# Attention block on one core: the row maxima's matmuls regrouped, three in a step and a round of four after every fourth

## The chip, the core and the metric

The kernel runs on one core of a Trainium2 chip. A time is the device time of one execution in microseconds. All engines of the core run at once: TensorE (matmuls; "PE" in the profile, its weight loads "PEld"), VectorE (DVE), ScalarE (ACT), GpSimd (POOL) and SyncE (SP, which issues most of the transfers). Each takes its instructions in the order of its program and waits at semaphores for the others.

## The reference

A transformer block with conditioning, two sequences of 2048 rows, width 512, 16 heads of 32:

```python
h = _ln(x) * (1.0 + scale_msa) + shift_msa
q = (h @ Wq + bq).reshape(B, L, H, DH)
k = (h @ Wk + bk).reshape(B, L, H, DH)
v = (h @ Wv + bv).reshape(B, L, H, DH)
scores = jnp.einsum('blhe,bshe->bhls', q, k)
A = jax.nn.softmax(scale * scores, axis=-1)
out = jnp.einsum('bhls,bshd->blhd', A, v)
x = x + gate_msa * (out @ Wo + bo)
h2 = _ln(x) * (1.0 + scale_mlp) + shift_mlp
m = jax.nn.gelu(h2 @ W1 + b1, approximate=False) @ W2 + b2
return x + gate_mlp * m
```

The change touches the scores, the softmax and the product with `v` only.

## The kernel before

Three stages: layer norm and the projections to q, k, v (to about 370 us), attention over 32 heads (16 of each sequence; to about 1975 us), then the output projection and the MLP. The projections and k and q are kept as a high and a low half, so that a product has three or more matmuls.

**A head of attention.** `G` is 32 heads, `NT` 16 steps. A step `t` takes 128 keys (on the partitions) against all 2048 queries (four quarters of 512, `r` = 0 to 3). For every quarter there is one score tile, S0 to S3, 128 x 512 in one bank of PSUM. It is the sum of four matmuls, its parts p0 to p3: high by high (line 1373), low by high (1375), high by low (1377), and minus the maximum of each query (1382). Each uses 32 rows of TensorE's array, quarter `r` the row group `r`, so that up to four of different quarters run together. ScalarE then takes the exponential of S0 to S3 (line 888), four a step. TensorE multiplies the probabilities of the step before by `v` ("values", line 1397) into bank 7.

**Max tiles.** The maximum of a query must be known before its exponentials. So in each step the kernel also computes score tiles of the next head the other way round (queries on the partitions, high halves only): the max tiles M0 to M3 (`max_tile`, line 1361), one matmul each, again in row group `r`. VectorE reduces each to one column of `part_max` (`quad`, line 1096); after the last of a head it reduces these columns to the row maxima and transposes them (lines 1043, 1049), and SyncE puts them in place for the next head.

**Sums.** The softmax's denominators are column sums of the probabilities. GpSimd adds up eleven of the sixteen tiles (`pool_tiles`: 0, 1, 3, 4, 6, 7, 9, 10, 12, 13, 14), twenty additions a head (line 737). TensorE sums the other five (2, 5, 8, 11, 15) and GpSimd's total, with four matmuls against ones each (line 1386): six groups a head, after the values, in steps 3, 6, 9, 12, in step 0 of the next head, and in step 4. ScalarE copies each out (line 866) and stores it. In step 0 it first copies the output of the head before (line 854), which waits for the same sums group. In step 8 VectorE makes the reciprocals of the denominators of the head before (lines 1106, 1108), after the step's reductions.

**Order in a step (TensorE).** Five slots of four matmuls of different row groups:
slot 0: p0 of S0 and S1, M2, M3; slot 1: p1 of S0 and S1, p0 of S2 and S3; slot 2: p2, and p1; slot 3: p3, and p2; slot 4: M0, M1, p3 of S2 and S3. Then values, then a sums group if the step has one. VectorE reduces in the order M2, M3, M0, M1.

**Banks.** Scores, max tiles and sums share seven banks of PSUM. `bank_table` (lines 87 to 131) walks the program in TensorE's order with estimated times of release (`until`, in units of its own) and gives each tile the bank that comes free first. It is a table made ahead; at run time the first matmul into a bank waits for what read it last (`bank_free`): `exp_ok` (ScalarE's exponential), `a_max` (VectorE's reduction) or `sums_ok` (ScalarE's copy). In the table of the head I looked at (head 10), M1 always gets the bank of M2 of the same step.

```python
elif kind == "M":
    pe.wait_ge(a_max, n)
```

Of the kernel before, what the change touches and what calls it, by code (L numbers as in the profile page):

```python
# [21 lines left out]
ALU = mybir.AluOpType  # L22
ACT = mybir.ActivationFunctionType
AX = mybir.AxisListType
# [10 lines left out]
TT = CH // P  # L35
CPB = L // CH
NCHUNK = B * CPB
G = B * H
NT = L // P
NQ = L // CH  # L40
# [7 lines left out]
FILLS = NQ * NT  # L48
LEAD = 3
FIRST_QUADS = 4  # L50
# [36 lines left out]
def bank_table():  # L87

    step, group = 11.7, 3.7
    until = {"S": (8, 10, 12, 14), "M": (11, 13, 6, 8), "D": 16}
    free = [0] * BANKS
    last = [None] * BANKS
    count = {"S": 0, "M": FIRST_FILLS, "D": 0}
    last[BANKS - 1] = ("M", FIRST_FILLS - 1)

    def use(kind, at, banks):
        bank = min(banks, key=lambda b: free[b])  # L100
        free[bank] = at
        before = last[bank]
        count[kind] += 1
        last[bank] = (kind, count[kind])
        return bank, before, count[kind]

    now = 0
    heads = []
    for g in range(G):
        steps = []  # L110
        for t in range(NT):
            tail = g == G - 1
            banks = range(BANKS)
            uses = {"max": [None] * NQ, "scores": [None] * NQ, "sums": []}
            for pair, others in ((0, 1), (2, 3)), ((2, 3), (0, 1)):
                for r in pair:
                    uses["scores"][r] = use("S", now + until["S"][r], range(3 + r, 4 + r) if tail else banks)
                if (g or t) and g < G - 2 or g == G - 2 and t < NT - LEAD:
                    for r in others:
                        uses["max"][r] = use("M", now + until["M"][r], banks)  # L120
            owner = g if t else g - 1
            groups = [(owner, pe_tiles(owner).index((t - 1) % NT))] if owner >= 0 and (t - 1) % NT in pe_tiles(owner) else []
            if g and t == ACC_STEP:
                groups.append((g - 1, ND - 1))
            for n, (o, d) in enumerate(groups):
                uses["sums"].append((o, d, *use("D", now + until["D"] + 2 * n, range(2, 3) if tail else banks)))
            now += step + group * len(groups)
            steps.append(uses)
        heads.append(steps)
    end = [(G - 1, d, *use("D", now, range(2, 3))) for d in (ND_MOST - 2, ND_MOST - 1)]  # L130
    return heads, end
# [8 lines left out]
def block_kernel(nc, x, cT, wq, wk, wv, wo, w1, w2, wada, bqT, bkT, b1T, badaT, bada, bv, bo, b2, out):  # L140
# [8 lines left out]
    with ExitStack() as ctx:  # L149
# [11 lines left out]
        ps = ctx.enter_context(nc.psum_tensor("ps", [P, 8, 512], F32))  # L161
# [39 lines left out]
        sums = [view(work, at, CH) for at in (3072, 1024)]  # L201
# [93 lines left out]
        a_mm = sem("a_mm")  # L295
# [651 lines left out]
        def _(dve):  # L947
# [89 lines left out]
            def row_maxima(g):  # L1037
                dve.wait_ge(a_max, (g + 1) * FILLS)
                if not isinstance(g, int) or g:
                    dve.wait_ge(maxT_ok, g)  # L1040
                else:
                    dve.wait_ge(zero_ok, 1)
                nc.vector.tensor_reduce(row_max[:, 0:NT], part_max[:], AX.X, ALU.max).then_inc(max_ok, 1)

            def transpose_max(g):
                dve.wait_ge(max_ok, g + 1)
                if not isinstance(g, int) or g:
                    dve.wait_ge(maxT_in, g * (16 * MAX_PIECES))
                nc.vector.transpose(max_T[:], row_max[:]).then_inc(maxT_ok, 1)
# [39 lines left out]
            chunk(NCHUNK - 1, 1, CPB - 1, nxt=False, nxt2=False, max_after=FIRST_MAX[NCHUNK - 1], max_at=MAX_AT_7)  # L1089
            assert next(fills, None) is None  # L1090

            def quad(uses, g, q):

                for r, (bank, _, n) in zip((2, 3, 0, 1), uses):
                    dve.wait_ge(a_mm, n)
                    nc.vector.tensor_reduce(part_max[:, r * TT + q // NQ, q % NQ:q % NQ + 1], ps[:, bank, :], AX.X, ALU.max).then_inc(a_max, 1)  # L1096
                if q == FILLS // NQ - 1:
                    row_maxima(g)
                    transpose_max(g)

            def denominators(g):

# [6 lines left out]

            def head(g, between={}):  # L1110

                q = g * (FILLS // NQ) + (LEAD if g else FIRST_QUADS)
                for t, uses in enumerate(USES[g]):
                    if uses["max"][0]:
                        quad([uses["max"][r] for r in (2, 3, 0, 1)], 1 + q // (FILLS // NQ), q % (FILLS // NQ))
                        q += 1
                    if t == STEP_RECIP and g:
                        denominators(g - 1)
                    if t in between:
                        between[t]()  # L1120
# [107 lines left out]
        def _(pe):  # L1228
# [126 lines left out]
            def max_tile(g, q, r, use):  # L1355


                bank_free(use)
                u = g % HI_BUF
                at = slice(r * DH, (r + 1) * DH)  # L1360
                nc.tensor.matmul(ps[:, use[0], :], q_hi[u][at, q // NQ * P:(q // NQ + 1) * P],  # L1361
                                 k_hi[u][at, q % NQ * CH:(q % NQ + 1) * CH], start=True, stop=True).then_inc(a_mm, 1)
# [48 lines left out]

            def head(g, between={}):

                per_head = FILLS // NQ
                q = g * per_head + (LEAD if g else FIRST_QUADS)
                pe.wait_ge(lo_in[g % TWO], (g // TWO + 1) * (16 * LOADS_LO))
                for t, uses in enumerate(USES[g]):
                    scores, tops = uses["scores"], uses["max"]
                    if tops[0] and q % per_head == 0:
                        ahead = 1 + q // per_head  # L1420
                        pe.wait_ge(hi_in[ahead % HI_BUF], (ahead // HI_BUF + 1) * (16 * LOADS_HI))
                    for part in range(5):
                        if part < 4:
                            score_part(g, t, 0, part)
                            score_part(g, t, 1, part)
                        if part:
                            if part == 4 and tops[0]:
                                for r in (0, 1):
                                    max_tile(1 + q // per_head, q % per_head, r, tops[r])
                            score_part(g, t, 2, part - 1)  # L1430
                            score_part(g, t, 3, part - 1)
                        elif tops[0]:
                            for r in (2, 3):
                                max_tile(1 + q // per_head, q % per_head, r, tops[r])
                    if tops[0]:
                        q += 1
                    if t:
                        values(g, t - 1)
                    elif g:
                        values(g - 1, NT - 1)  # L1440
                    take_sums(uses["sums"])
                    if t in between:
                        between[t]()
# [114 lines left out]
```

## Time and profile before

| | |
|---|---|
| median of 3 runs | 2422.54 us (2421.5 to 2427.32) |
| profiled execution: time | 2425.6 us |
| its span | 2423.8 us |
| mean granted TensorE clock | 0.989 |
| busy TensorE / VectorE / ScalarE / GpSimd | 2362.5 / 1743.6 / 1403.8 / 1656.4 us |
| attention, 700 to 1680 us (980 us): the same four | 978.5 / 809.4 / 744.4 / 943.6 us |

The busy time of TensorE counts matmuls that run together and their modelled ends, so it does not show how tightly its queue is filled; for that one reads when each instruction starts. Idle time is shown as [idle, what ended it]. The attention stage repeats the same pattern head for head, so a few steps stand for all.

### The profile page before, as it was taken

To read this page: it belongs to the slowest core of one execution; us is meant where nothing else is said; L and a number is where in the kernel's file an instruction comes from. 1 tells how busy PE (TensorE), PEld (TensorE's weight loads), DVE (VectorE), ACT (ScalarE), POOL (GpSimd) and SP (SyncE) were. 2 spreads that over 40 slices of the span, in tenths; PEclk is the share of its full clock that TensorE was granted. 3 is DMA by queue.
4 is the path that set the end of the run, shared out by engine and by line. 5 is a ranking of instruction groups with operands and counts; after the bars stand their busy time and mean duration, and the time that the engine had idled before them with its cause. 6 is when DMAs were issued, how large, how long until landed. Compare 5 with 4: busy or idle time off the path is not lost.

```text
span 2423.8 us, 48535 instructions
## 1 busy us (share of the span) xinstructions
PE 2362.5 (97%) x19312; PEld 1341.3 (55%) x19312; DVE 1743.6 (72%) x2866; ACT 1403.8 (58%) x2591; POOL 1656.4 (68%) x776
## 2 busy tenths in 40 slices
PE   6999989999999999999999999999999889999998
PEld 4787764444444444444444444444444458888887
DVE  5445747888888888888888888888888656655653
ACT  3232216777777777777777777777777642222221
POOL 0000017999999999999999999999999842233320
PEclk9999999999999999999999999999999989999999
DMA  8666463332333323232323223322323223222200
GB/s 282 192 195 185 133 165 76 69 82 65 70 80 72 75 64 82 57 82 56 80 57 82 56 67 70 75 63 60 77 59 75 68 70 94 70 70 70 70 35 35
DMA packets 208845, 211.14 MB, mean 87 GB/s; under 512 B 116253, under 2 KB 149021, under 8 KB 199081
## 3 DMA queue, kind: packets, MB, share of 16 engines
q1 hardware_dynamic: 206338, 206.41, 32.8%
q8 instruction: 152, 2.49, 0.4%
q10 hardware_dynamic: 2280, 1.63, 0.3%
q14 instruction: 75, 0.61, 0.1%
HBM read 147.11 MB, written 60.59 MB: 86 GB/s over the span
## 4 chain that ended last, share of the span: by engine, by line
PE 91%; ACT 2%; DMA 2%; DVE 2%; issue 2%; SPq 1%; POOL 0%; ACTq 0%; POOLq 0%; DVEq 0%
PE ps L1397 21%; PE ps L1258 19%; PE ps L1373 11%; PE ps L1361 11%; PE ps L1501 7%; PE ps L1386 7%; PE ps L1375 6%; PE ps L1377 5%; PE ps L1382 3%; DMA q_lo<-work 1%; PE ps L1267 1%; ACT work L866 1%; PE ps L1299 1%; DVE acts_r L1136 0%; ACT work L802 0%
## 5 line engine op out<-in xcount | busy, mean ns | idle before, releaser
L1096 DVE TENSOR_REDUCE part_max<-ps 128x1 f32<-128x512 f32 x1968 | 1221.5, 682 | 265.2 <-PE ps L1361 265.2
L888 ACT ACTIVATE work<-ps 128x512 f32<-128x512 f32 x2048 | 1057.8, 603 | 324.1 <-PE ps L1382 281.9
L737 POOL TENSOR_TENSOR work<-work 128x1024 f32<-128x1024 f32 x314 | 739.8, 2412 | 37.8 <-ACT work L888 37.3
L737 POOL TENSOR_TENSOR gate<-gate,work 128x1024 f32<-128x1024 f32 x288 | 675.1, 2404 | 14.4 <-ACT work L888 14.4
L1397 PE MATMUL ps<-work 128*32 128x512 f32 x4096 | 546.4, 605 | 0.1
L1361 PE MATMUL ps<-acts_r 32*128 32x512 f32 x1328 | 412.6, 471 | 3.3 <-ACT work L888 1.8
L1258 PE MATMUL ps<-acts_r,weights_r 128*128 128x512 f32 x1536 | 382.7, 399 | 4.6 <-DVE acts_r L1013 3.9
L1258 PEld LDWEIGHTS ps<-acts_r,weights_r 128*128 128x128 f32 x1536 | 291.1, 192 | 70.8 <-issue 6.4
L1373 PEld LDWEIGHTS ps<-acts_r 32*128 32x128 f32 x1408 | 141.2, 182 | 305.1 <-DVE part_max L1096 175.2
L1373 PE MATMUL ps<-acts_r 32*128 32x512 f32 x1408 | 291.4, 466 | 1.4 <-issue 0.8
L1375 PE MATMUL ps<-acts_r 32*128 32x512 f32 x1408 | 252.7, 394 | 0.0
L1361 PEld LDWEIGHTS ps<-acts_r 32*128 32x128 f32 x1328 | 179.8, 182 | 109.9 <-DVE part_max L1096 89.1
L941 ACT ACTIVATE work<-ps,b_sb 128x512 f32<-128x512 f32 x64 | 44.2, 690 | 333.0 <-PE ps L1258 333.0
L709 POOL TENSOR_TENSOR var_eps<-var_eps,mv 128x4 f32<-128x4 f32 x16 | 3.2, 202 | 338.5 <-DVE mv L991 338.5
L1382 PE MATMUL ps<-acts_r,minus_r 1*128 1x512 f32 x1024 | 228.8, 441 | 0.0
L1382 PE MATMUL ps<-m_odd,minus_r 1*128 1x512 f32 x1024 | 225.6, 438 | 0.0
L761 POOL TENSOR_TENSOR work<-work,gate_b 128x512 f32<-128x512 f32 x60 | 86.4, 1470 | 169.8 <-DMA work<-in_x 149.4
L1258 PE MATMUL ps<-weights_r,acts_r 128*128 128x512 f32 x768 | 191.6, 401 | 8.9 <-DVE acts_r L1136 8.9
L1361 PE MATMUL ps<-acts_r,w_r 32*128 32x512 f32 x640 | 198.6, 470 | 0.8
L1386 PE MATMUL ps<-work,ones 128*32 128x512 f32 x1432 | 187.3, 595 | 0.0
L1377 PE MATMUL ps<-w_r,acts_r 32*128 32x512 f32 x1024 | 184.6, 394 | 0.0
L1501 PE MATMUL ps<-w_r,acts_r 128*128 128x512 f32 x768 | 184.4, 391 | 0.0
(95 smaller groups left out, 2808.1 us busy)
## 6 DMA issues: line engine op xcount, KB each, us to landing
acts_r<-k_hi SPq DMA_DIRECT2D x130, 256.0 KB, 4.7
acts_r<-k_lo SPq DMA_DIRECT2D x129, 256.0 KB, 4.7
work<-in_x SPq DMA_DIRECT2D x16, 1024.0 KB, 6.1
q_hi<-work SPq DMA_DIRECT2D x32, 256.0 KB, 3.1
q_lo<-work SPq DMA_DIRECT2D x32, 256.0 KB, 3.5
k_hi<-work SPq DMA_DIRECT2D x32, 256.0 KB, 2.6
k_lo<-work SPq DMA_DIRECT2D x32, 256.0 KB, 3.2
v_rows<-work SPq DMA_DIRECT2D x32, 256.0 KB, 2.0
```

What stands on the lines that cost most here:

```text
L737: nc.gpsimd.tensor_tensor(acc[:, at], first, prob[:, t % RING, at], ALU.add).then_inc(add_ok, 1)
L888: nc.scalar.activation(prob[:, t % RING, j * CH:(j + 1) * CH], ps[:, bank, :], ACT.Exp, scale=SCALE).then_inc(exp_ok, 1)
L1096: nc.vector.tensor_reduce(part_max[:, r * TT + q // NQ, q % NQ:q % NQ + 1], ps[:, bank, :], AX.X, ALU.max).then_inc(a_max, 1)
L1258: mm = nc.tensor.matmul(o, lhs(s, kk), rhs(r, kk), start=(kk == 0 and s == r), stop=(kk == KC - 1 and s == 1))
L1361: nc.tensor.matmul(ps[:, use[0], :], q_hi[u][at, q // NQ * P:(q // NQ + 1) * P], k_hi[u][at, q % NQ * CH:(q % NQ + 1) * CH], start=True, s ...
L1373: nc.tensor.matmul(o, k_hi[u][at, keys], q_hi[u][at, :], start=True, stop=False)
L1375: nc.tensor.matmul(o, k_lo[w][at, keys], q_hi[u][at, :], start=False, stop=False)
L1377: nc.tensor.matmul(o, k_hi[u][at, keys], q_lo[w][at, :], start=False, stop=False)
L1382: nc.tensor.matmul(o, minus_r[row, :], m_row[w][row, :], start=False, stop=True).then_inc(b_mm, 1)
L1386: mm = nc.tensor.matmul(ps[j * DH:(j + 1) * DH, bank, :], ones[:, 0:DH], src(j), start=True, stop=True)
L1397: mm = nc.tensor.matmul(ps[j * DH:(j + 1) * DH, O_BANK, :], v_sb[g % TWO][:, t, :], prob[:, t % RING, j * CH:(j + 1) * CH], start=(t == 0) ...
L1501: mm = nc.tensor.matmul(ps[:, 4 + t, :], g_r[:, f % 4, s, t * P:(t + 1) * P], w2_r[:, r, f, :], start=(f == 0 and s == r), stop=(f == FB - ...
```

## The change

The four max tiles of a step (a "round" in the code; rounds are numbered through all heads, `FIRST_QUADS` of them made ahead) become three: tile `r` equal to the round's number modulo 4 is left out. In a step of a head after the first the round's number modulo 4 is (t + 3) modulo 4: steps 1, 5, 9, 13 leave out M0, steps 2, 6, 10, 14 M1, steps 3, 7, 11, 15 M2, steps 0, 4, 8, 12 M3. In the latter the four tiles left out in the last four steps follow after the values and ahead of a sums group, as four matmuls together, here called L0 to L3. VectorE takes them after the step's three; row maxima and, in step 8, denominators follow them. The number of max tiles is the same. The bank table is made anew by the same rule, with estimates for L0 to L3. The short description of the change also speaks of TensorE summing tile 7 in place of 8; the code leaves `pool_tiles` as it was.

```diff
@@ bank_table
-            uses = {"max": [None] * NQ, "scores": [None] * NQ, "sums": []}
+            uses = {"round": None, "max": [None] * NQ, "late": [], "scores": [None] * NQ, "sums": []}
+            if (g or t) and g < G - 2 or g == G - 2 and t < NT - LEAD:
+                uses["round"] = next(rounds)
...
-                if (g or t) and g < G - 2 or g == G - 2 and t < NT - LEAD:
+                if uses["round"] is not None:
                     for r in others:
-                        uses["max"][r] = use("M", now + until["M"][r], banks)
+                        if r != uses["round"] % NQ:
+                            uses["max"][r] = use("M", now + until["M"][r], banks)
+            if uses["round"] is not None and uses["round"] % NQ == NQ - 1:
+                uses["late"] = [use("M", now + 15 + 2.8 * r, banks) for r in range(NQ)]
+                now += 2.6
...
@@ VectorE, head
-                    if uses["max"][0]:
-                        quad([uses["max"][r] for r in (2, 3, 0, 1)], 1 + q // (FILLS // NQ), q % (FILLS // NQ))
-                        q += 1
+                    if uses["round"] is not None:
+                        q = uses["round"] % NT
+                        for r in (2, 3, 0, 1):
+                            if uses["max"][r]:
+                                tile_max(q, r, uses["max"][r])
+                        for r, use in enumerate(uses["late"]):
+                            tile_max(q - (NQ - 1) + r, r, use)
+                        if q == NT - 1:
+                            row_maxima(1 + uses["round"] // NT)
+                            transpose_max(1 + uses["round"] // NT)
...
@@ TensorE, head
                     if t:
                         values(g, t - 1)
                     elif g:
                         values(g - 1, NT - 1)
+
+                    for r, use in enumerate(uses["late"]):
+                        max_tile(ahead, q - (NQ - 1) + r, r, use)
                     take_sums(uses["sums"])
```

What stands in TensorE's queue at two places of head 10. A row is line, operation, tile written and read, and in brackets the semaphore that it waits for; L1373 is the first part of a score, L1361 a max tile, L1397 the values, L1386 a sums group (after: L1383, L1371, L1407, L1396). First, the end of step 8 and the begin of step 9, before:

```order
L1397 MATMUL ps<-work 32x512 [waits exp_ok]
L1397 MATMUL ps<-work 32x512 x3
L1373 MATMUL ps<-acts_r 128x512 [waits exp_ok]
L1373 MATMUL ps<-acts_r 128x512 [waits a_max]
L1361 MATMUL ps<-acts_r,w2_r 128x512 [waits exp_ok]
L1361 MATMUL ps<-acts_r,w2_r 128x512 [waits a_max]
L1375 MATMUL ps<-acts_r 128x512 x2
L1373 MATMUL ps<-acts_r 128x512 [waits exp_ok]
L1373 MATMUL ps<-acts_r 128x512 [waits a_max]
```

And after:

```order
L1407 MATMUL ps<-work 32x512 [waits exp_ok]
L1407 MATMUL ps<-work 32x512 x3
L1371 MATMUL ps<-acts_r,w2_r 128x512 [waits a_max]
L1371 MATMUL ps<-acts_r,w2_r 128x512 [waits exp_ok] x2
L1371 MATMUL ps<-acts_r,w2_r 128x512 [waits a_max]
L1383 MATMUL ps<-acts_r 128x512 [waits exp_ok]
L1383 MATMUL ps<-acts_r 128x512 [waits a_max]
L1371 MATMUL ps<-acts_r,w2_r 128x512 [waits exp_ok]
L1371 MATMUL ps<-acts_r,w2_r 128x512 [waits a_max]
L1385 MATMUL ps<-acts_r 128x512 x2
L1383 MATMUL ps<-acts_r 128x512 [waits a_max] x2
L1387 MATMUL ps<-w2_r,acts_r 128x512 x2
```

The round L0 to L3 stands between the values and step 9, and both first parts of S2 and S3 (the last but one row) now wait for reductions: by the table S2 for that of L1, S3 for that of M2 of step 9 itself. Before, S3 waited for M0 of step 8.

Second, the begin of step 1, behind the sums group of step 0, before:

```order
L1386 MATMUL ps<-work,ones 32x512 x3
L1373 MATMUL ps<-acts_r 128x512 [waits a_max]
L1373 MATMUL ps<-acts_r 128x512 [waits exp_ok]
L1361 MATMUL ps<-acts_r,w2_r 128x512 [waits exp_ok]
L1361 MATMUL ps<-acts_r,w2_r 128x512 [waits a_max]
L1375 MATMUL ps<-acts_r 128x512 x2
L1373 MATMUL ps<-acts_r 128x512 [waits exp_ok]
L1373 MATMUL ps<-acts_r 128x512 [waits a_max]
```

And after:

```order
L1396 MATMUL ps<-work,ones 32x512 x3
L1383 MATMUL ps<-acts_r 128x512 [waits a_max]
L1383 MATMUL ps<-acts_r 128x512 [waits exp_ok]
L1371 MATMUL ps<-acts_r,w2_r 128x512 [waits a_max] x2
L1385 MATMUL ps<-acts_r 128x512 x2
L1383 MATMUL ps<-acts_r 128x512 [waits sums_ok]
L1383 MATMUL ps<-acts_r 128x512 [waits a_max]
```

M2 and M3 wait for reductions (L0 and L1), S2 in slot 1 for the copy of the sums group of step 0, S3 for L2. Before, the wait for that copy stood at M0, in slot 4.

## Rows read from the trace of the kernel before

**Rows 1.** Waits, 700 to 1700 us: engine, line, releaser: us, times, longest.

```profile
PEld ps L1361 <- DVE part_max L1096: 88.4, 283, 0.5
```

**Rows 2.** One step in order of time: start, us, engine, line, operation, tiles, count, [idle].

```profile
1004.20 0.50 PE L1373 MATMUL ps<-acts_r 32*128 32x512 f32 x2
...
1004.54 0.40 PE L1375 MATMUL ps<-acts_r 32*128 32x512 f32 x2
...
1004.75 2.48 DVE L1096 TENSOR_REDUCE part_max<-ps 128x1 f32<-128x512 f32 x4 [0.24 <-PE ps L1361]
...
1005.00 0.40 PE L1382 MATMUL ps<-acts_r,minus_r 1*128 1x512 f32 x2
...
1005.24 0.75 PE L1361 MATMUL ps<-acts_r,w_r 32*128 32x512 f32 x2
1005.49 0.18 PEld L1361 LDWEIGHTS ps<-acts_r,w_r 32*128 32x128 f32 x1 [0.30 <-DVE part_max L1096]
...
1005.50 0.49 PE L1382 MATMUL ps<-acts_r,minus_r 1*128 1x512 f32 x2
1005.92 1.06 PE L1397 MATMUL ps<-work 128*32 128x512 f32 x8
...
1006.92 0.49 PE L1373 MATMUL ps<-acts_r 32*128 32x512 f32 x2
```

**Rows 3.** VectorE: the cost of one reduction; denominators in step 8; row maxima.

```profile
L1096 DVE TENSOR_REDUCE part_max<-ps 128x1 f32<-128x512 f32 x1968 | 1221.5, 682 | 265.2 <-PE ps L1361 265.2
...
1038.12 0.31 DVE L1106 TENSOR_REDUCE den_c<-sums_c 128x16 f32<-128x96 f32 x1
...
1038.64 2.41 DVE L1096 TENSOR_REDUCE part_max<-ps 128x1 f32<-128x512 f32 x4
...
1050.11 0.22 DVE L1043 TENSOR_REDUCE row_max<-part_max 128x16 f32<-128x64 f32 x1
1050.37 0.21 DVE L1049 STREAM_TRANSPOSE max_T<-row_max 128x32 f32<-128x32 f32 x1
```

**Rows 4.** GpSimd's additions in a row; copies of three heads' outputs, first and last start.

```profile
1031.25 32.77 POOL L737 TENSOR_TENSOR work<-work 128x1024 f32<-128x1024 f32 x14 [0.46 <-ACT work L888]
...
L854 ACT ACTIVATE work<-ps x3: 598/600/600, 1013.4 to 1111.6; 128x512 f32<-128x512 f32 x3
```

**Rows 5.** Sums groups and ScalarE's copies, step 0 to 1 and step 3.

```profile
1012.24 1.04 PE L1386 MATMUL ps<-work,ones 128*32 128x512 f32 x8
1013.22 0.50 PE L1373 MATMUL ps<-acts_r 32*128 32x512 f32 x2
...
1013.35 0.60 ACT L854 ACTIVATE work<-ps 128x512 f32<-128x512 f32 x1 [0.30 <-PE ps L1386]
1013.85 0.59 ACT L866 ACTIVATE work<-ps 128x512 f32<-128x512 f32 x1
...
1020.65 1.06 PE L1397 MATMUL ps<-work 128*32 128x512 f32 x8
1021.53 1.04 PE L1386 MATMUL ps<-work,ones 128*32 128x512 f32 x8
...
1022.64 0.60 ACT L866 ACTIVATE work<-ps 128x512 f32<-128x512 f32 x1 [0.36 <-PE ps L1386]
```

**Rows 6.** Step 8: S2's first part after a hold, and its second.

```profile
1035.68 0.50 PE L1373 MATMUL ps<-acts_r 32*128 32x512 f32 x2
...
1035.78 0.19 PEld L1375 LDWEIGHTS ps<-acts_r 32*128 32x128 f32 x2
...
1036.01 0.39 PE L1375 MATMUL ps<-acts_r 32*128 32x512 f32 x2
```

**Rows 7.** The start of attention: a long hold; windows (last: PEclk, DMA share, GB/s).

```profile
370.11 0.51 PE L1373 MATMUL ps<-acts_r 32*128 32x512 f32 x4 [0.83 <-issue]
...
373.31 0.79 PE L1361 MATMUL ps<-acts_r 32*128 32x512 f32 x1 [1.75 <-ACT work L888]
...
372.00:379.00 7.00, 5.69 (x33) 2.70 (x37) 2.27 (x4) 4.78 (x9) 2.19 (x1) 0.54 0.77 173
```

More of the change, by code:

```diff
@@ L107, in bank_table @@
     now = 0
+    rounds = iter(range(FIRST_QUADS, G * NT))
     heads = []
@@ L1090, in _, with tile_max @@
             assert next(fills, None) is None
[L1092 to L1099, printed above, removed]
+            def tile_max(q, r, use):
+                bank, _, n = use
+                dve.wait_ge(a_mm, n)
+                nc.vector.tensor_reduce(part_max[:, r * TT + q // NQ, q % NQ:q % NQ + 1], ps[:, bank, :], AX.X, ALU.max).then_inc(a_max, 1)
             def denominators(g):
@@ L1110, in head @@
             def head(g, between={}):
-                q = g * (FILLS // NQ) + (LEAD if g else FIRST_QUADS)
                 for t, uses in enumerate(USES[g]):
-                    if uses["max"][0]:
-                        quad([uses["max"][r] for r in (2, 3, 0, 1)], 1 + q // (FILLS // NQ), q % (FILLS // NQ))
-                        q += 1
+                    if uses["round"] is not None:
[8 more added lines that the diff above has]
+                            transpose_max(1 + uses["round"] // NT)
                     if t == STEP_RECIP and g:
@@ L1412, in head @@
             def head(g, between={}):
-                per_head = FILLS // NQ
-                q = g * per_head + (LEAD if g else FIRST_QUADS)
                 pe.wait_ge(lo_in[g % TWO], (g // TWO + 1) * (16 * LOADS_LO))
@@ L1418, in head @@
                     scores, tops = uses["scores"], uses["max"]
-                    if tops[0] and q % per_head == 0:
-                        ahead = 1 + q // per_head
+                    ahead, q = (1 + uses["round"] // NT, uses["round"] % NT) if uses["round"] is not None else (0, 0)
+                    if ahead and q == 0:
                         pe.wait_ge(hi_in[ahead % HI_BUF], (ahead // HI_BUF + 1) * (16 * LOADS_HI))
@@ L1426, in head @@
                         if part:
-                            if part == 4 and tops[0]:
+                            if part == 4:
                                 for r in (0, 1):
-                                    max_tile(1 + q // per_head, q % per_head, r, tops[r])
+                                    if tops[r]:
+                                        max_tile(ahead, q, r, tops[r])
                             score_part(g, t, 2, part - 1)
                             score_part(g, t, 3, part - 1)
-                        elif tops[0]:
+                        else:
                             for r in (2, 3):
-                                max_tile(1 + q // per_head, q % per_head, r, tops[r])
-                    if tops[0]:
-                        q += 1
+                                if tops[r]:
+                                    max_tile(ahead, q, r, tops[r])
                     if t:
```

## The prediction

> **What bounds the kernel now.** I read the waits first, then one step on all engines in order of time, then the length of a head. In the waits of the middle stretch [rows 1] TensorE's weight loads for max tiles (line 1361) are held 283 times by VectorE, 88.4 us in all, 0.3 us each. One step [rows 2] shows which: S0 of the step starts at 1004.20; the p1 slot follows 0.34 later, p3 of S0 at 1005.00 (0.80), M0 at 1005.24 (1.04). M1 should go with M0, but sits in the bank of M2 of the same step, whose reduction began at 1004.75 and needs 0.68 [rows 3]; M1 goes at 1005.49, and since TensorE issues in order p3 of S2 and S3 goes at 1005.50. Values follow 0.42 later (1005.92), the next step 1.00 after that: 2.72 us. Without the hold it is 1.04 + 0.42 + 0.99 = 2.45. So TensorE's in-order stream sets the end, lengthened by bank waits. Behind it VectorE is close: four reductions take 2.48 [rows 2], 0.60 apart. GpSimd is closer: 14 additions take 32.77, 2.35 each [rows 4]; a head has 20, 47.1 us of a head of (1111.6 - 1013.4) / 2 = 49.1 [rows 4]. A head cannot get shorter than 47.1.
>
> **What the change removes.** With three max tiles in a step, none sits in the bank of M2 of its own step when M1 comes: I went through the bank table of head 10, and in it M1 never follows M2 of the same step. Sixteen holds of 0.27 go, 4.3 us a head, and with them 0.4 of scattered waits in the head before (49.1 less 16 steps of 2.72 and six sums groups of 0.86). The 0.86: values to sums is 0.88, sums to the next S0 0.98 [rows 5], together 1.86 in place of 0.99. A head without any bank wait would be 16 x 2.45 + 6 x 0.86 = 44.4. A slot with three matmuls in place of four is taken at the same price: the slots are spaced 0.23 to 0.24 by each row group's own next matmul.
>
> **What it adds: the round.** Four matmuls of their own, after values, in steps 0, 4, 8 and 12 of a head (123 rounds in the kernel). TensorE changes from values to 32-row matmuls (0.99), from these to the sums group (0.43, as from slot 4 to values [rows 2]), instead of 0.88 straight: 0.54 more in steps 0, 4 and 12, where a sums group follows. Step 8 has none: 0.34 (the distance of the first two slots [rows 2]). Sum 1.96 a head.
>
> **What it adds: waits behind the round.** VectorE gets seven tiles in a round's step. L0's reduction starts 0.54 after the round (as M2's after S0 [rows 2]), the others 0.60 apart, each ready 0.68 after its start and its bank taken 0.06 later (reduction from 1004.75, M1 at 1005.49). The step that follows wants these banks early, in slots 0 and 1, and TensorE's queue holds all score parts behind. Counted from S0 of the following step:
> Step 5 (after step 4): M3 waits for L1, 0.34; S2 for the sums group's copy, 0.81 (sums matmul to copy 1.11, copy 0.60 [rows 5], S0 0.97 after the sums); S3 for L2, 0.94. Then p1 at 1.27, p2 1.50, p3 1.74 (0.33 after a hold, as from 1035.68 to 1036.01 [rows 6], then 0.23 and 0.24). M1 waits for L3, 1.54, and is hidden. Step 3.16, 0.71 over the clean 2.45.
> Step 13: the round is 0.14 later against S0, S3 at 1.08: 3.30, 0.85 over. VectorE then also does the row maxima (0.22 and 0.21 [rows 3]); its M1 is late enough to hold S3 of step 14 until 0.76: 0.53 over.
> Step 1: ScalarE copies the head's output before the sums (1013.35, then 1013.85 to 1014.44, which is 1.22 after S0 at 1013.22 [rows 5]). Before, M0 in slot 4 wanted this bank (1.04 at the earliest); now S2 in slot 1 does, and goes at 1.30: p3 2.10, step 3.52, 1.07 over.
> The round's own steps want S3's bank from an exponential of the step before (ready 0.52 to 0.57 into the step instead of 0.34): 0.28 to 0.34 in steps 0, 8 and 12, and 0.14 in step 4 where the sums wait for S2's exponential. With small rests 1.1. Together 1.1 + 0.71 + 0.85 + 0.53 + 1.07 = 4.3.
> For the 0.33 after a hold there is another reading. In the row, the load for p1 of S2 starts at 1035.78, 0.10 after its matmul p0, and the matmul comes at 1036.01 [rows 6]. The Trainium skill ("TensorE: Matmul & The Clock Gate", "Step-by-step: what each phase is for") says that weight loads are pulled ahead of matmuls in flight where row groups don't conflict or into a background buffer; by it the queue would restart at 0.23, and eight holds a head would cost 0.8 less, 25 us in all. I stay with the row.
>
> **What it adds: one long wait.** In step 9 the table gives S3 (slot 1) the bank of M2 (slot 0) of the same step, as it gave M1 that bank before; but now the hold comes in slot 1, and M2's reduction stands behind the whole round and the denominators. The round of step 8 goes 2.79 after its S0 and S0 of step 9 at 3.13. Reductions: L0 3.33, L3 5.13, then the denominators in place of 5.73, which cost 0.52 (1038.12 to 1038.64 [rows 3]), M2 at 6.25, done 6.93. S3 goes at 6.99, 3.86 into step 9; until then all that is queued (p2, p3, values, sums) waits. p3 4.66, values 5.09, sums 5.97, step 6.94 instead of 2.45 + 0.86 = 3.31: 3.63 over. The table has this in step 9 of every head from 0 to 30.
>
> **Sum.** 44.4 + 1.96 + 4.3 + 3.63 gives 54.2 a head (with the pieces unrounded) for 49.1: 5.1 more. Steps with max tiles are 492 (1968 reductions by 4), 30.75 heads: 157 us. The profiled execution is 2423.8 of span and 2425.6 in time; 2425.6 + 157 = 2583. The median of the runs is 3 lower.
>
> **The clock.** TensorE idles 1.8 us in each step 9 (S2's first matmul, begun at 1.54 and 0.50 long, to 3.86). After a wait of 1.75 (with another of 0.83 shortly before) the clock fell: 372 to 379 ran at 0.54 [rows 7], and lost 7 x 0.46 = 3.2 us. The holds of 0.3 never lowered it. The new wait is nearest to the 1.75, but without a second one near it, so between 0 and 31 x 3.2 = 99 us; I take a third, 33. That makes 2616 of the profiled, **2613** as a median.
>
> **Rivals.**
> *The intended gain.* If banks were free by the time they are wanted after a round, a head would be 44.4 + 2.0 = 46.4, and GpSimd's 47.1 would decide; some 47.5 with its own waits, 1.6 less x 30.75: 2374. It needs the step 9 hold to be no hold; VectorE's order and the table speak against it. Chance 0.06.
> *Only step 9 counts.* The smaller waits hide beneath one another and the restart costs 0.23: 44.4 + 2 + 3.6 and about 1 is 51, 1.9 more a head, 2480 to 2530. It is slower all the same; it would turn to no change only where the small waits and half of step 9's went. 0.12.
> *The clock falls in every step 9.* 2583 + 99 = 2682, median about 2680; slow matmuls would then show in every head. 0.15.
> *The change as its words say.* Tile 7 is not summed by TensorE: the list of tiles is untouched, the sums group stays in step 9. If it moved to step 8, the table would hand S3 of step 9 the bank of L2, the 3.6 would shrink to about 1.3, and the time to about 2510. The code decides against it, and it has no chance of its own.
> *A second queue.* GpSimd, held back by the long step 9, makes ScalarE wait in steps 10 to 15. In my walk its addition for tile 14 ends 2 us before it is wanted again, so 0.04, above 2700.
>
> **How the numbers follow.** Forecast (step 9 long, small waits as walked, the clock down in some heads) 0.59; the rest as above, and 0.04 for something between gain and no change. Range 2510 to 2690: from the second rival's upper part to the clock's, beyond which lie 0.06 + 0.04 + 0.04 and a few hundredths of the second. A measurement of this kernel tells 0.3% (7 us) from no change: faster 0.08, within 0.04, slower 0.88.
>
> **What would show it.** Heads 54 us long or more by the copies of the output; one step in a head of 7 us, with TensorE's line for S3 held by VectorE near 2.3 us; clean steps of 2.45 (2, 7, 10) with no hold at M1; steps 1, 5, 13 of 3.2 to 3.5; steps 0 and 12 near 4.1; GpSimd's share down from 96% of a head to 87%. VectorE's reductions keep 0.60. Wrong, if step 9 is under 5 us, if the matmuls of a round don't go together, or if clean steps stay at 2.72.

## The result, and the profile after

The changed kernel takes 2603.54 us by the median of five runs, the kernel before 2422.54, also by five: a ratio of 1.0744 with an interval of [1.0721, 1.0767]. It is 181 us slower; 2613 was forecast. One of the five executions, the profiled one, took 3724.65 us at a mean granted clock of 0.555, which was down from some 34 us on, long before the changed part, for a reason that the runs don't show; it stands in no comparison. The profile shown here is of another run of the same kernel (e1_after, 2602.19 us median of 4).

| | before | after (e1_after) |
|---|---|---|
| span of the profiled execution | 2423.8 | 2601.6 |
| mean granted clock | 0.989 | 0.967 |
| a head, by the copies of the output | 49.1 | 54.7 |
| VectorE idle before reductions, all | 265.2 | 419.5 |
| GpSimd idle before additions, all | 52 | 200 |

The length of a head, from the first and the last of eighteen copies of a head's output (answers [rows 4]), (1473.6 - 544.4) / 17 = 54.66:

```profile
L861 ACT ACTIVATE work<-ps x18: 597/597/599, 544.4 to 1473.6; 128x512 f32<-128x512 f32 x18
```

The reductions in the list of groups (answers [rows 3]): as many, each as long (684 ns against 682), but with more idle time ahead of them.

```profile
L1103 DVE TENSOR_REDUCE part_max<-ps 128x1 f32<-128x512 f32 x1968 | 1251.1, 684 | 419.5 <-PE ps L1371 415.9
```

The waits from 700 to 1700 us. Before the change a score's first part (line 1373) was held by VectorE like this:

```profile
PEld ps L1373 <- DVE part_max L1096: 170.2, 203, 0.8
```

After it (line 1383) the weight loads are held for about as long in total, but single holds are up to 2.1 us long. Matmuls now wait idle for them as well (last row), for which there is no row before the change. The max tiles' holds (answers [rows 1]) go from 283 to 127:

```profile
PEld ps L1383 <- DVE part_max L1103: 180.7, 212, 2.1
...
PEld ps L1371 <- DVE part_max L1103: 74.7, 127, 0.8
...
PE ps L1383 <- DVE part_max L1103: 31.6, 18, 1.8
```

And step 9 of one head, from the round of step 8 to the first score of step 10 (start, us, engine, line, [idle]):

```profile
1005.02 1.06 PE L1407 MATMUL ps<-work 128*32 128x512 f32 x8
...
1006.02 0.51 PE L1371 MATMUL ps<-acts_r 32*128 32x512 f32 x4
...
1006.38 0.50 PE L1383 MATMUL ps<-w_r,acts_r 32*128 32x512 f32 x2
1006.54 2.48 DVE L1103 TENSOR_REDUCE part_max<-ps 128x1 f32<-128x512 f32 x4 [0.35 <-PE ps L1371]
...
1007.89 0.50 PE L1383 MATMUL ps<-w_r,acts_r 32*128 32x512 f32 x1
1008.95 0.30 DVE L1110 TENSOR_REDUCE den_c<-sums_c 128x16 f32<-128x96 f32 x1
...
1009.45 1.22 DVE L1103 TENSOR_REDUCE part_max<-ps 128x1 f32<-128x512 f32 x2
...
1010.14 0.50 PE L1383 MATMUL ps<-w_r,acts_r 32*128 32x512 f32 x1 [1.75 <-DVE part_max L1103]
...
1011.27 1.91 PE L1407 MATMUL ps<-work 128*32 128x512 f32 x8
...
1012.93 1.95 PE L1396 MATMUL ps<-work,ones 128*32 128x512 f32 x8
...
1014.81 0.50 PE L1383 MATMUL ps<-w_r,acts_r 32*128 32x512 f32 x2
```

Read it with the forecast's walk beside it. The round starts 1.00 after the values (1005.02, 1006.02) and S0 of step 9 0.36 after the round. VectorE reduces L0 to L3 from 1006.54, makes the denominators from 1008.95 and begins M2 at 1009.45; S3's first part goes at 1010.14, 3.76 into the step (3.86 by the walk), after 1.75 of idle time. Values and sums, 1.06 and 1.04 long elsewhere [rows 2, 5], take 1.91 and 1.95: the clock is down. The windows say so (PE, PEld, DVE, ACT, POOL, then clock):

```profile
1006.38:1010.14 3.76, 1.92 (x12) 0.74 (x9) 3.56 (x8) 0.44 (x1) 2.99 (x2) 1.00 0.29 43
1010.14:1014.81 4.67, 4.67 (x28) 1.28 (x29) 1.22 (x2) 2.07 (x4) 2.67 (x2) 0.63 0.04 5
1014.81:1019.71 4.90, 4.90 (x59) 2.35 (x56) 3.65 (x6) 3.88 (x8) 4.41 (x3) 1.00 0.01 2
```

Step 9 takes 8.43 us in all; in the kernel before it took 3.71.

### The profile page after: what moved, and what is told of

The parts are those of the page before. It is cut to its first block, busy times and chain, and to the rows that moved or that the text cites. A ratio compares the mean times of both kernels' runs of the same rounds, so it can differ in the third digit from the quotient of the medians.

```text
span 3722.8 us, 48535 instructions
## 1 busy us (share of the span) xinstructions
PE 3611.8 (97%) x19312; PEld 1443.3 (39%) x19312; DVE 1749.0 (47%) x2866; ACT 1407.9 (38%) x2591; POOL 1646.1 (44%) x776
## 4 chain that ended last, share of the span: by engine, by line
PE 95%; DVE 3%; issue 1%; ACT 1%; DMA 0%; POOL 0%; SPq 0%; ACTq 0%; POOLq 0%
PE ps L1268 24%; PE ps L1407 22%; PE ps L1396 8%; PE ps L1383 8%; PE ps L1512 8%; PE ps L1392 7%; PE ps L1385 7%; PE ps L1387 4%; PE ps L1371 3%; DVE part_max L1103 2%; PE ps L1277 1%; PE ps L1309 1%; ACT work L873 1%; PE ps L1247 0%; DVE rec_c L1112 0%
## 5 line engine op out<-in xcount | busy, mean ns | idle before, releaser
L1103 DVE TENSOR_REDUCE part_max<-ps 128x1 f32<-128x512 f32 x1968 | 1267.9, 685 | 1025.8 <-PE ps L1371 1023.6
L895 ACT ACTIVATE work<-ps 128x512 f32<-128x512 f32 x2048 | 1057.5, 602 | 875.0 <-PE ps L1392 781.6
L744 POOL TENSOR_TENSOR work<-work 128x1024 f32<-128x1024 f32 x314 | 737.9, 2374 | 444.2 <-ACT work L895 444.2
L1407 PE MATMUL ps<-work 128*32 128x512 f32 x4096 | 852.6, 931 | 0.0
L1268 PE MATMUL ps<-acts_r,weights_r 128*128 128x512 f32 x1536 | 620.4, 580 | 4.2 <-DVE acts_r L1020 3.4
L1371 PE MATMUL ps<-acts_r 32*128 32x512 f32 x1328 | 433.0, 561 | 9.5 <-DVE part_max L1103 7.9
L1268 PEld LDWEIGHTS ps<-acts_r,weights_r 128*128 128x128 f32 x1536 | 338.1, 222 | 249.6 <-issue 143.3
L1383 PE MATMUL ps<-acts_r 32*128 32x512 f32 x1408 | 355.6, 551 | 46.7 <-DVE part_max L1103 37.0
L1383 PEld LDWEIGHTS ps<-acts_r 32*128 32x128 f32 x1408 | 140.4, 211 | 566.9 <-DVE part_max L1103 230.2
L1385 PE MATMUL ps<-acts_r 32*128 32x512 f32 x1408 | 357.0, 561 | 0.0
L1396 PE MATMUL ps<-work,ones 128*32 128x512 f32 x1432 | 309.2, 957 | 0.0
L1512 PE MATMUL ps<-w_r,acts_r 128*128 128x512 f32 x768 | 307.6, 579 | 0.0
L1268 PE MATMUL ps<-weights_r,acts_r 128*128 128x512 f32 x768 | 306.1, 575 | 0.2 <-issue 0.2
L1387 PE MATMUL ps<-w_r,acts_r 32*128 32x512 f32 x1024 | 262.0, 565 | 0.0
L1387 PE MATMUL ps<-acts_r 32*128 32x512 f32 x1024 | 257.7, 563 | 0.0
L873 ACT ACTIVATE work<-ps 128x512 f32<-128x512 f32 x195 | 116.5, 598 | 286.5 <-PE ps L1396 286.5
L1371 PEld LDWEIGHTS ps<-acts_r 32*128 32x128 f32 x1328 | 149.7, 190 | 182.8 <-DVE part_max L1103 133.0
```

Of the source, the lines that this page charges most:

```text
L744: nc.gpsimd.tensor_tensor(acc[:, at], first, prob[:, t % RING, at], ALU.add).then_inc(add_ok, 1)
L895: nc.scalar.activation(prob[:, t % RING, j * CH:(j + 1) * CH], ps[:, bank, :], ACT.Exp, scale=SCALE).then_inc(exp_ok, 1)
L1268: mm = nc.tensor.matmul(o, lhs(s, kk), rhs(r, kk), start=(kk == 0 and s == r), stop=(kk == KC - 1 and s == 1))
L1383: nc.tensor.matmul(o, k_hi[u][at, keys], q_hi[u][at, :], start=True, stop=False)
L1385: nc.tensor.matmul(o, k_lo[w][at, keys], q_hi[u][at, :], start=False, stop=False)
L1387: nc.tensor.matmul(o, k_hi[u][at, keys], q_lo[w][at, :], start=False, stop=False)
```

## The experiments

All runs are compared with runs of the kernel before on the same chip (2423.7 to 2426.8 us by the median). TensorE's mean clock stands beside each time, since it turned out to matter.

**1. The changed kernel, for its profile (e1_after).**

> The changed kernel as it is, for a profile. My theory: a head is 54.2 us by the copies of the output, against 49.1; step 9 takes 6.9, with S3's first part held by VectorE until 3.9 into the step; steps 0 and 12 take 4.1, step 1 3.5, step 5 3.2, clean steps 2.45; the clock falls during or just behind step 9 in a good part of the heads. Rival: the time is in the rounds themselves (a second change between the two kinds of matmuls), about 1.3 us in each of steps 0, 4, 8 and 12, and step 9 is under 5. Rival on the clock: it falls in every head (about 3.4 us or more at half speed a head), then the walk without the clock is some 40 us too long elsewhere.

Measured: 2602.19 us, 1.0734 [1.0716, 1.0752], clock 0.967. A head is 54.66; from S0 to S0, from step 9 of one head to step 8 of the next: step 9 8.43, step 10 2.36, 11 2.54, 12 3.97, 13 3.15, 14 2.87, 15 2.35, 0 4.12, 1 3.41, 2 2.48, 3 3.24, 4 4.17, 5 2.92, 6 3.34, 7 2.37, 8 3.12. Every walked step except 9 is within 0.25 us. The rounds' own price is as walked: where a sums group follows (step 0), values at 1033.74, the round 1.00 later, the sums 0.43 after it.

```profile
1033.74 1.06 PE L1407 MATMUL ps<-work 128*32 128x512 f32 x8
1034.74 0.51 PE L1371 MATMUL ps<-acts_r 32*128 32x512 f32 x4
1035.17 1.07 PE L1396 MATMUL ps<-work,ones 128*32 128x512 f32 x8
1036.17 0.50 PE L1383 MATMUL ps<-acts_r 32*128 32x512 f32 x2
...
1037.44 0.50 PE L1383 MATMUL ps<-acts_r 32*128 32x512 f32 x2 [0.34 <-ACT work L873]
```

The last row is S2 of step 1, held until 1.27 into the step by ScalarE's copy of the sums (1.30 walked). So the first rival (the rounds cost it, and step 9 stays under 5) falls. The rival on the clock stands: the clock fell behind every step 9 (the falls lie 54.6 us apart).

**2. Another rule for the banks (e3_bank).** In step 9 S3 now follows L2 instead of its own step's M2. The rule also moves others there (M1 follows L3 instead of L2, the sums group M2 instead of M3), and some tiles of steps 3, 8 and 10 get another bank.

```diff
-        bank = min(banks, key=lambda b: free[b])
+        fresh = [b for b in banks if not (last[b] and last[b][0] in "MS" and last[b][1] > step_start[last[b][0]])]
+        bank = min(fresh or banks, key=lambda b: free[b])
...
+            step_start.update(count)
```

> Only the bank table's rule is changed: no tile takes a bank that another tile of the same step had before. S3 of step 9 then follows L2 instead of M2 of its own step; all other steps keep their waits. My theory: step 9 falls from 6.9 to 5.2 (M1 still waits for L3 and the denominators' neighbours), 31 x 1.7 = 53 us less, and the idle stretch of 1.8 us shrinks, so the clock is back near the 0.989 of before and some 30 to 60 us more go: 2490 to 2525. Rival (the rounds themselves cost it): less than 20 us go. Rival on the clock (it falls for another reason than step 9's wait): mean clock stays at 0.967 and only about 53 go.

Measured: 2500.9 us, 1.0316 [1.0299, 1.0333], clock 0.987, a head (1461.3 - 535.0) / 18 = 51.46. S3 goes at 2.10 into step 9 instead of 3.76. So 101 us hang on the table's new rule, nearly all of it, to judge by the holds, on the neighbour of S3. Neither rival fits: more than 20 and more than 53 went, and the clock came back as the wait went (it still fell twice between 500 and 1700 us, at 1025.8 and 1541.2).

**3. The list of tiles as the change's words have it (e4_tile7).**

```diff
-    return [0, 1, 3, 4, 6, 7, 9, 10] + ([12, 13, 14] if g < G - 1 else [])
+    return [0, 1, 3, 4, 6, 8, 9, 10] + ([12, 13, 14] if g < G - 1 else [])
```

> The list of tiles as the change's words have it: TensorE sums tile 7, GpSimd adds 8, so a sums group stands in step 8 behind the round and none in step 9. By the table S3 of step 9 then waits for L2. My theory: step 8 takes 4.1, step 9 about 3.3 to 3.7, a head 52.0; 31 x 2.1 = 65 us less than the changed kernel, and the clock is back, another 30 to 60: 2480 to 2510. It stays slower than the kernel before, since steps 1, 5, 9 and 13 all wait for the round's reductions. Rival (the intended gain, with this list the scheme works): under 2422.

Measured: 2486.31 us, 1.026 [1.0242, 1.0277], clock 0.988, a head 50.96. With the sums group in step 8 the table doesn't give S3 of step 9 the bank of M2, and VectorE has 0.9 us more to catch up. It stays slower than before, as expected: no hold is longer than 0.8 any more, but 256 of them are left at the scores' first parts.

```profile
PEld ps L1383 <- DVE part_max L1103: 189.3, 256, 0.8
```

**4. Three max tiles and no round (e5_noround).** A quarter of the max tiles is left out.

```diff
-            if uses["round"] is not None and uses["round"] % NQ == NQ - 1:
+            if False:
```

> Three max tiles in a step and no round: a quarter of the max tiles is left out (max_tile and its reduction), so the subtracted maxima are not all true maxima. It prices the part of the change that should give. My theory: the hold of M1 goes in all steps, TensorE's walk gives 44.4 us a head, and GpSimd's 47.1 decides: heads of 47.1 to 47.5, 2360 to 2375 us, with ScalarE waiting for GpSimd. Rival (a slot with three matmuls saves nothing and another wait takes the hold's place): heads stay near 49, 2415 to 2425.

Measured: 2374.26 us, 0.98 [0.9784, 0.9817], clock 0.982. A head is (1464.8 - 516.4) / 20 = 47.42, just over the 47.1 of GpSimd's additions:

```profile
L861 ACT ACTIVATE work<-ps x21: 598/601/602, 516.4 to 1464.8; 128x512 f32<-128x512 f32 x21
```

and in the waits from 700 to 1700 us ScalarE waits for GpSimd to free the tiles that it writes:

```profile
ACT work L895 <- POOL gate L744: 23.9, 20, 2.6
...
ACT work L895 <- POOL work L744: 18.0, 18, 2.6
```

Three max tiles a step and no round are worth 49 us and no more, because GpSimd comes next. (A quarter of the reductions is gone too, so the removed hold at M1 by itself is worth at most this.) The rounds with all that hangs on them cost 2602 - 2374 = 228.

**5. Denominators after step 10 (e2_recip).**

```diff
-                    if t == STEP_RECIP and g:
+                    if t == STEP_RECIP + 2 and g:
```

> The changed kernel with the denominators (0.5 us of VectorE) moved from behind step 8 to behind step 10. Nothing else is moved; the table is the same. My theory: they stand in VectorE's queue between the round's reductions and that of M2, so the hold of S3 in step 9 ends 0.5 earlier (3.2 instead of 3.8 into the step) and TensorE idles 1.2 us there instead of 1.75. That is 31 x 0.5 = 16 us less, 2586; if the clock's fall hangs on the length of that idle stretch and 1.2 is too short for it, it stays up and another 31 x 1.7 = 52 go: 2534. Rival (the denominators run beside): no change, 2602. Between 2586 and 2534 I expect the second, with little certainty.

Measured: 2577.06 us, 1.0627 [1.0609, 1.0644], clock 0.973. Half a microsecond of VectorE in the wrong place in its queue is paid in full: S3 goes at 3.30 into the step instead of 3.76.

```profile
1051.03 0.49 PE L1383 MATMUL ps<-acts_r 32*128 32x512 f32 x2
...
1054.33 0.49 PE L1383 MATMUL ps<-acts_r 32*128 32x512 f32 x1 [1.30 <-DVE part_max L1103]
```

The time lies between the two expected ones, because the clock still fell in 23 of 29 heads. The falls lie mostly 54.6, 54.6 and 105.8 us apart, and 105.8 spans two heads: three heads of four, not two of three as the expectation of e11_fill4 below has it. That gives 16 for the denominators and about 10 for the six heads without a fall; 25 was measured.

**6. The round's reductions over half their columns (e6_half).** The other half of L0 to L3 is left out of the maxima.

```diff
-                nc.vector.tensor_reduce(part_max[...], ps[:, bank, :], AX.X, ALU.max).then_inc(a_max, 1)
+                nc.vector.tensor_reduce(part_max[...], ps[:, bank, 0:n_of], AX.X, ALU.max).then_inc(a_max, 1)
...
-                            tile_max(q - (NQ - 1) + r, r, use)
+                            tile_max(q - (NQ - 1) + r, r, use, 256)
```

> The changed kernel with the reductions of L0 to L3 over 256 of the 512 columns, so that half of each of these tiles is left out of the maxima; the matmuls are whole, table and order are the same. My theory: what the steps behind a round wait for is VectorE's queue, so each of these four costs 0.33 instead of 0.60; S3 in step 9 goes 1.1 earlier (2.7), the idle stretch is 0.7 and the clock stays up (1.7 more), the hold in step 14 goes (0.5), steps 5 and 13 shorten by 0.2 each as the sums group's copy (0.81) then decides: 3.6 a head, 31 heads, 110 us less: 2485 to 2500. Rival (the round's matmuls and the changes between matmul kinds are the cost): less than 30 less.

Measured: 2531.01 us, 1.0427 [1.041, 1.0445], clock 0.973: 71 less, where 100 to 115 were expected. The mechanism shows: four reductions in 1.42 instead of 2.48, S3 at 2.71 into the step, 2.7 walked. S2 went earlier too, so that 1.22 us of idle time were left instead of 0.7.

```profile
1026.04 0.50 PE L1383 MATMUL ps<-acts_r 32*128 32x512 f32 x2
1026.22 1.42 DVE L1103 TENSOR_REDUCE part_max<-ps 128x1 f32<-128x256 f32 x4 [0.36 <-PE ps L1371]
...
1028.75 0.68 PE L1383 MATMUL ps<-acts_r 32*128 32x512 f32 x1 [1.22 <-DVE part_max L1103]
```

What is missing is the clock. Idle stretches of the same 1.22 us had both outcomes: in nine heads in a row (from 458 us) the clock stayed up, in the next seven it fell, then it stayed up in five and fell in seven. The copies of the output in heads of the first kind and of the second, and a window behind step 9 in each (the clock is the third figure from the end):

```profile
L861 ACT ACTIVATE work<-ps x9: 597/598/599, 483.4 to 893.8; 128x512 f32<-128x512 f32 x9
...
L861 ACT ACTIVATE work<-ps x5: 597/598/599, 1001.1 to 1219.3; 128x512 f32<-128x512 f32 x5
...
870.00:875.00 5.00, 5.00 (x55) 1.83 (x47) 2.69 (x5) 3.32 (x7) 3.30 (x2) 1.00 0.04 6
1084.00:1091.00 7.00, 7.00 (x51) 2.65 (x44) 1.83 (x4) 2.74 (x6) 4.68 (x2) 0.55 0.00 1
```

A head without a fall is (893.8 - 483.4) / 8 = 51.3, that is 3.4 less than the changed kernel's 54.7, close to the 3.6 expected. A head with one is (1219.3 - 1001.1) / 4 = 54.6. So a fall here costs 3.3 us, about twice as much as in the changed kernel, since the clock stays down longer.

**7. Rounds of two after every second step (e7_pairs).**

```diff
+EVERY = 2
...
-            if uses["round"] is not None and uses["round"] % NQ == NQ - 1:
-                uses["late"] = [use("M", now + 15 + 2.8 * r, banks) for r in range(NQ)]
-                now += 2.6
+            if uses["round"] is not None and uses["round"] % EVERY == EVERY - 1:
+                uses["late"] = [use("M", now + LATE_AT + 2.8 * r, banks) for r in range(EVERY)]
+                now += LATE_NOW
```

> Rounds of two tiles after every second step instead of four after every fourth: VectorE then never has more than two reductions behind a round, but TensorE changes twice as often (eight rounds a head, 0.34 or 0.54 each, 3.6 us instead of 2.0). By the same walk with its bank table a head is 50.7 to 51.2: the waits behind the rounds shrink (steps 1, 5 and 13 to 2.5 to 2.8 in place of 3.0 to 3.4) and the long wait of step 9 is gone, 2475 to 2495. Rival (fewer reductions behind a round remove the waits entirely and GpSimd's 47.1 decides): under 2400. Rival (a round's own price decides): about the changed kernel, 2600.

Measured: 2488.39 us, 1.0255 [1.0238, 1.0272], clock 0.992. Within what was expected. It costs what the scheme with tile 7 costs; by the walk that is twice the changes between kinds of matmuls in place of the long queue, which no run separates.

**8. Rounds of four with table, tiles and denominators set for them (e9_best).**

```diff
-    return [0, 1, 3, 4, 6, 7, 9, 10] + ([12, 13, 14] if g < G - 1 else [])
+    return [0, 1, 2, 4, 5, 6, 9, 10] + ([12, 13, 14] if g < G - 1 else [])
...
-    step, group = 11.7, 3.7
-    until = {"S": (8, 10, 12, 14), "M": (11, 13, 6, 8), "D": 16}
+    step, group = 14.06, 5.32
+    until = {"S": (10.3, 8.7, 12.0, 13.3), "M": (9.8, 11.4, 7.6, 8.0), "D": 19.0}
...
-                uses["late"] = [use("M", now + 15 + 2.8 * r, banks) for r in range(NQ)]
-                now += 2.6
+                uses["late"] = [use("M", now + LATE_AT + 0.6 * r, banks) for r in range(EVERY)]
+                now += LATE_NOW
...
-                    if t == STEP_RECIP and g:
+                    if t == STEP_RECIP + 2 and g:
```

(`EVERY` is 4, `LATE_AT` 17.9 and `LATE_NOW` -0.5.)

> The change's rounds of four with everything around them set for them: TensorE sums tiles 3, 7, 8, 11, 15 (a free step behind fewer of the rounds), other estimates in the bank table (step 14.06, group 5.32, S 10.3 8.7 12 13.3, M 9.8 11.4 7.6 8.0, D 19, round 17.9 + 0.6 r), denominators behind step 10. By the same walk a head is about 50, 2440 to 2465: still slower than the kernel before, since of the 6.1 that a step without the hold gives back in a head (49.1 less 43.0), the rounds' matmuls take 2 and the waits behind four rounds 4 or more whatever the banks. Rival (a bad table was the whole trouble): under 2415.

Measured: 2458.91 us, 1.0135 [1.0119, 1.0152], clock 0.991. The best form of the scheme that I found is still 32 us slower than the kernel before (2426.82 on the same chip). No version that keeps all max tiles beat the kernel before.

**9. The stretch in step 9 filled with small matmuls (e10_fill, e11_fill4).** Eight or four copies of S2's first part ahead of it, 32 rows each.

```diff
+                            if t == 9 and part == 1 and uses["round"] is not None:
+                                bank_free(scores[2])
+                                for _ in range(8):
+                                    nc.tensor.matmul(ps[:, scores[2][0], :], k_hi[g % HI_BUF][2 * DH:3 * DH, t * P:(t + 1) * P],
+                                                     q_hi[g % HI_BUF][2 * DH:3 * DH, :], start=True, stop=True)
                             score_part(g, t, 2, part - 1)
```

> The changed kernel with eight matmuls more in each step 9, ahead of S2's first part and equal to it (they write the bank that it overwrites right after). They run from 1.5 to 3.3 into the step, when TensorE sits idle until S3 may go at 3.76; nothing waits for them. They price the clock by itself. My theory: the fall of the clock behind each step 9 comes from the idle 1.75 us and costs 1.7 a head; with the stretch filled the clock stays up and 31 x 1.7 = 52 us go, 2550, though there is more work. Rival (the fall has to do with something else, as the lighter steps around): clock still down in each head, 2602 or some us more.

> The same with four such matmuls: an idle stretch of some 0.8 us is left. My theory: 0.8 is too short to bring the clock down in most heads (1.30 did it in two heads of three in the run with the denominators moved), 2550 to 2560. Rival as before: 2602.

Measured: 2604.28 us, 1.0744 [1.0726, 1.0762], and 2604.33, 1.0751 [1.0733, 1.0769]; clocks 0.966 and 0.968. Both expectations of mine missed. The eight matmuls run where they should, TensorE is busy from 1008.76 to 1010.86, and the clock falls all the same, in all but two heads of e10_fill and of e11_fill4 (where 0.83 us of idle time is left):

```profile
1008.76 2.10 PE L1442 MATMUL ps<-w_r,acts_r 32*128 32x512 f32 x8
```

The windows around it:

```profile
1007.26:1011.50 4.24, 4.14 (x27) 2.56 (x26) 4.04 (x8) 0.43 (x1) 2.99 (x2) 1.00 0.10 12
1011.50:1015.60 4.10, 4.10 (x28) 0.83 (x20) 0.75 (x2) 2.06 (x4) 2.58 (x2) 0.58 0.00 0
```

The idle time alone is not the cause.

**10. The same stretch filled with full matmuls (e12_full).** As before, over all 128 rows.

```diff
-                                    nc.tensor.matmul(ps[:, scores[2][0], :], k_hi[g % HI_BUF][2 * DH:3 * DH, t * P:(t + 1) * P],
-                                                     q_hi[g % HI_BUF][2 * DH:3 * DH, :], start=True, stop=True)
+                                    nc.tensor.matmul(ps[:, scores[2][0], :], k_hi[g % HI_BUF][:, t * P:(t + 1) * P],
+                                                     q_hi[g % HI_BUF][:, :], start=True, stop=True)
```

> As the run with eight more matmuls in step 9, but each of them over all 128 rows of the array instead of 32. In that run TensorE's records show no idle stretch any more in step 9 and the clock fell all the same, so idle time by itself was not the cause. My theory now: a stretch in which matmuls use one row group of four does as little against the fall as an idle one; with full matmuls in the same place the clock stays up, and the 1.7 us a head behind step 9 go: about 2550. Rival (the fall has nothing to do with what TensorE does between 1.5 and 3.8 us of step 9, but with the waits before or behind): still one fall in each head, 2602.

Measured: 2550.51 us, 1.0522 [1.0504, 1.054], clock 0.988. The same instructions in number and length (2.11 against 2.10), in the same place, and the clock stays up behind them in every head from 411 us to the end of attention; values take 1.06 again:

```profile
1044.04 2.11 PE L1442 MATMUL ps<-acts_r 128*128 128x512 f32 x8
1046.08 0.72 PE L1383 MATMUL ps<-acts_r 32*128 32x512 f32 x2
...
1047.43 1.06 PE L1407 MATMUL ps<-work 128*32 128x512 f32 x8
1048.32 1.04 PE L1396 MATMUL ps<-work,ones 128*32 128x512 f32 x8
```

This prices the clock by itself: 2602.2 - 2550.5 = 52 us, 1.7 for each of 31 steps 9. S3 goes at 3.76 into the step as in the changed kernel (1046.30 after 1042.54), step 9 takes 6.75 instead of 8.43 (8.35 in most heads), and the other steps are as long as there. It also leaves a head of (1495.0 - 540.4) / 18 = 53.03 without the clock's part.

## Why the prediction was right, point by point

**The gain.** Right in kind. The hold of M1 is gone from the clean steps: steps 2, 7 and 10 are 2.48, 2.37 and 2.36 long where 2.45 were walked. The 0.09 of step 10 (1014.81 to 1017.17) is a gap I had taken from the wrong place: with no max tile held in slot 4, values follow the last parts 0.33 to 0.35 later, not 0.42. In a whole head the walk was 1.2 us too long (54.2 against 53.0), in small pieces; the largest, of 0.2 each, are in steps 5, 9 and 12. The limit behind it, GpSimd's 47.1 a head, was right to 0.3 (experiment 4).

**The round.** Right: 1.00 and 0.43 around it where a sums group follows, 0.36 to the next step in step 8 (0.34 walked).

**The waits behind the round.** Right in place and nearly in size: step 1 3.41 (3.52), step 5 2.92 (3.16), step 13 3.15 (3.30), step 14 2.87 (2.98); step 0 4.12 (4.14), step 12 3.97 (4.14), step 8 3.12 (3.13), step 4 4.17 (3.99). The second part after a held first part came 0.34 later in the first case one can look at (S3's second part at 1010.48 after 1010.14), as in [rows 6]. By the Trainium skill's page "TensorE: Matmul & The Clock Gate" ("Step-by-step: what each phase is for") a weight load goes ahead of matmuls in flight where it may; the load for that second part stands after the held matmul of its row group in this trace too (that row group's load starts at 1010.24). So the row was the right choice; after the hold in step 1 the second part comes 0.34 later as well (1037.78 after 1037.44).

**The long wait.** Right: S3 of step 9 at 3.76 (3.86), and with the clock up (experiment 10) the step is 6.75 (6.94). Experiment 5 shortens the queue before M2's reduction by the denominators, experiment 6 by the reductions, and S3 moved by what each took out: 0.46 for 0.5, and 1.05 for 1.06. Experiment 2 takes the assignment away, and S3 goes at 2.10.

**The clock.** The step that failed, twice, with errors that partly cancelled. I took a price of 3.2 in a third of the heads, 33 us; it is 1.7 in every head, 52 us. In the row of the start of attention [rows 7] the clock was down twice as long as behind step 9 (the 3.2 came back only in experiment 6, in ten of its heads). The share was a guess between nearest rows. And the reason I gave, idle time, is not what decides by itself: experiment 9 shows a filled stretch and the same fall, experiment 6 the same idle stretch with a fall and without.

**The sum.** Walk 157 forecast, 126 measured (experiment 10 as a whole over before; by its heads it is 53.0 - 49.1 = 3.9, times 30.75, 121). Clock 33 forecast, 52 measured. Together 190 forecast, 178 measured. The walk was 31 too high and the clock 19 too low, so it is in part luck that the forecast came as near as 9 us. Where the loss comes from, by the runs: no round would be 49 below before; the clock is 52 above; the assignment in step 9 without the clock is 101 - 52 = 49 at least (in experiment 2 step 9 keeps a shorter wait); the other 127 are the rounds' own matmuls and reductions and the waits behind them. The 49 gained and these 127 cannot be split further by these runs, because a part of what the rounds cost is hidden in heads that GpSimd would hold at 47.4.

**The rivals.** The intended gain exists, but only for a kernel without rounds. "Only step 9 counts" was wrong: with it mended, 2501 remain, 77 over before. "The clock falls in every head" was right in its condition and twice too high in its price. The change as its words say gives 2486, where I had said about 2510.

## What to carry to other kernels

Before leaving a queue's tight spot, ask where the work goes: four reductions in a row behind a round make every early bank of the next step late, while the same four spread over a step fit. In an in-order queue, the position of a wait prices it: the bank of M2 of the same step cost 0.27 us when M1 took it in the last slot. When S3 took it in the second slot behind a round, with everything behind it standing, step 9 was 3.5 longer than a step 3, which also has a sums group (6.75 against 3.24), and about 1.6 of this (49 us in 31 heads) went with another bank. And a bank table made with estimates should be searched for tiles that come early in a step and follow one of their own step, since such a wait includes all that the releasing engine has queued.

## What the runs showed of the hardware that I had not expected

TensorE's clock fell from its upper level (2.4 GHz) to the lower (1.2 GHz) behind a stretch in which it had matmuls of a single 32-row group back to back (eight in 2.10 us, no idle time on record), as it does behind an idle stretch; with eight matmuls of all 128 rows in 2.11 us in the same place it did not fall. Two runs differ in nothing else, and by 54 us (2604.28, 2550.51). So a busy TensorE in the profile does not mean that the clock is safe. Idle stretches of 1.75 us brought it down in every head, of 1.30 in 23 of 29 (experiment 5), of 1.22 in 14 of 30 (experiment 6), there in runs of heads, with the same instructions around them. So the length of the stretch alone does not decide; what does is open, and so is what four row groups at once would have done in place of all 128 rows.
